# Cross-attention kernel: row statistics on ScalarE instead of VectorE, one constant row on GpSimd

## Chip, cores, metric

One core of a Trainium2 chip runs the program; the time is the device time of one execution in microseconds. Three runs of the kernel before took 2336.01, 2340.18 and 2342.96 us: median 2340.18 us. The profiled execution took 2341.09 us, of which its profile spans 2339.3 us.

## What is computed

Two layers on `x` and a context `ctx`, both 8 batches of 512 rows by 2048 channels, all float32. This study concerns the first layer and its input normalization:

```
xn = (x - mean(x)) / sqrt(var(x) + eps)          # over the 2048 channels of a row
corr = ifft(fft(xn) * conj(fft(ctx))).real       # along the 512 rows, per channel
w, idx = top_k(corr, 12);  w = softmax(w)        # per channel
out[l] = sum_i w[i] * ctx[min(idx[i] + l, 511)]  # "clamped shift" of ctx
x = x + out
```

A second layer (layer norm, 64 experts of rank 8, top 16 gate) follows on tiles of 128 rows. The change does not touch it.

## The kernel before

The transforms along the rows are written as matrix products with fixed tables. The work is cut into 32 groups: 8 batches (`B`) times 4 quarters of 512 channels (`GPB` = 4). A software pipeline runs 33 steps `i`; every engine has a hand-written order of work within `body(k, r, a, b, f, s)`, `i = 4k + 3 + r`. In step `i` the forward half handles group `i` (flag `a`) and the backward half handles group `i-1` (flag `b`). So there is no planner: what an engine does next is the next line of its own `body`, and semaphores tie the engines together.

**TensorE in a step** (from L627): the ctx transform of group `i` (`ctx_cyclic`, L533, then `ctx_negacyclic`, L557, four pairs of matmuls n = 0 to 3 into two evacuation banks), between them the x transform (`x_spectrum`, L543); the turned weights of group `i-1` (L568); the correlation of tiles 0 and 1 (L585); the weight spectrum of group `i-1` in four blocks (L601); the correlation of tiles 2 and 3; the 12 `out_row` matmuls (L623). Of these, `out_row(0, 2)` waits for `dc_put`.

**VectorE in a step** (L913 to L990): four products for the x spectrum; `evac_sin(0)` and `evac_sin(1)` (L847), which empty an evacuation bank that TensorE wants back for n = 3 and for the turned weights; the constant row ("dc", L923: row 0 of `v_cyc` gets `L * v_last`); four `w_lo`; the sums of tiles 0 and 1; the eight products of the weight spectrum; then the top-k of tiles 0 and 1, `choose` (L891) of them, the sums and top-k of tiles 2 and 3, the attention output and `choose_last`. `choose(t)` waits for the exponentials of ScalarE: `exp_done`.

**Row statistics.** A row's mean and variance must be there before its first quarter is normalized, so they are gathered two batches ahead: one quarter per step is loaded into `stat_in`, VectorE takes `bn_stats` of its four 128-row tiles (`statistics`, L736; two tiles after `evac_sin(0)`, two before the products of the weight spectrum), and in every fourth step (r = 3, that is i = 2, 6, ... 26; called a means step below) `means` (L742) aggregates them, ScalarE takes the root (`root`, L1082), VectorE inverts (`invert`, L775, after the second block's products) and GpSimd finishes `rstd` and `shift` (`normalizers`, L1316). ScalarE's `norm` (L1071) of group `i+2` waits for these in a means step. Steps from i = 27 on gather no statistics.

**ScalarE in a step** (L1153 to L1230): evacuations and negated copies, `w_hi`, the odd copies of tiles 0 and 1, `norm` of group `i+2`, then `dc_put` (L1205: the constant row into `r_f`, after GpSimd's third sum of products), then `big_exp` and `top_exp` of tiles 0 and 1 (L1144, L1148), the odd copies of tiles 2 and 3, `weigh`, and the copy of the attention output.

**GpSimd in a step** (L1358): the folds of the weights, first half of the x fold, the sums of products of the x spectrum, second half of the x fold (L1291, L1292), first op of the ctx fold (L1297), four sums of products of the weight spectrum, rest of the ctx fold.

**SyncE's queue** issues in order: x of group `i+2`, ctx of group `i+1`, its last row (`load_last`), `stat_in`, the store of the attention output.

The order on ScalarE that the change writes into:

```
                if i + 2 < GROUPS:
                    norm_inputs(k, r, 2)
                    norm(k, r, 2, range(LT))
                ...
                if b:
                    act.wait_ge(add_done, prod_w(i, 2) + 1)
                    act.wait_ge(dc_ready, i)
                    nc.scalar.activation(r_f[0:1, 0, :], ...).then_inc(dc_put, 1)
                if a:
                    for t in (0, 1):
                        big_exp(i, t)
```

Of the kernel before, what the change touches and what calls it, by code (L numbers as in the profile page):

```python
# [129 lines left out]
def build_program(nc, x, ctx, a_w, b_w, wq_w, keys, tables, out):  # L130
# [6 lines left out]
    with ExitStack() as st:  # L137
# [13 lines left out]
        def sem(name):  # L151
            return st.enter_context(nc.semaphore(name))


        ident, pace = sb("ident", [P, P]), sb("pace", [P, 32])
        bn_x, norm_x = sb("bn_x", [P, LT, GPB, 6]), [sb(f"norm_x{n}", [P, LT, 2]) for n in range(2)]
        rstd2, shift2 = sb("rstd2", [P, TT]), sb("shift2", [P, TT])
# [6 lines left out]
        xfs[1], vf = sb("xf1", [P, 4, CH]), sb("vf", [P, 4, CH])  # L164
        fwd, v_last = sb("fwd", [P, 13, P]), sb("v_last", [P, CH])
        v_cyc[0], v_neg[0] = sb("v_cyc0", [P, 6, CH]), sb("v_neg0", [P, 6, CH])
# [40 lines left out]
            sem("tables_loaded"), sem("fwd_loaded"), sem("tables_split"), sem("x0_half"))  # L207
        stat_loaded, stat_used = sem("stat_loaded"), sem("stat_used")
        norm_step, root_done, norm_ready = sem("norm_step"), sem("root_done"), sem("norm_ready")
        consts_set = sem("consts_set")  # L210
# [3 lines left out]
        evac_ready, evac_act, evac_dve, minus_done = sem("evac_ready"), sem("evac_act"), sem("evac_dve"), sem("minus_done")  # L214
        dc_ready, dc_put = sem("dc_ready"), sem("dc_put")
        w_hi_done, w_lo_done = sem("w_hi_done"), sem("w_lo_done")
# [137 lines left out]
        def _(sp):  # L354
# [28 lines left out]
            def body(k, r, a, b, f, s):  # L383
                i = 4 * k + 3 + r

                if i + 2 < GROUPS:
                    sp.wait_ge(pair_ready, pair_x(i, 1) + 1)
                    load_x(k, r, 2)
                if f:
                    sp.wait_ge(evac_ready, evac_neg(i, 3) + 1)  # L390
                    load_v(k, r, 1)
                    sp.wait_ge(dc_ready, i + 1)
                    load_last(k, r, 1)
                if is_step(i, 0):
                    sp.wait_ge(stat_used, LT * 2)
                    load_stat(k, r, stat_in[:], stat_loaded)
                if (i - 2) // GPB + 2 < B:
                    sp.wait_ge(stat_used, LT * (i + 3))
                    load_stat((i - 2) // GPB, (i - 2) % GPB, stat_in[:], stat_loaded)
                if is_step(i, GROUPS - 1):  # L400
                    last_group(i)
                if is_step(i, GROUPS):
                    last_step(i)
                if b:
                    sp.wait_ge(att_done, i)
                    sp.dma_start(at_group(att_t, k, r, -1), att_sb[:]).then_inc(stored, 16)
# [24 lines left out]
            def last_group(i):  # L431

                sp.wait_ge(stored, 16 * GPB)
                sp.wait_ge(pair_ready, pair_x(i - 1, 1) + 1)
                sp.wait_ge(stat_used, LT * (1 + GPB * (B - 1)))
                for h in range(2):
                    load_rows(0, 0, h)
                load_others(0, 0, 0)
                sp.wait_ge(v_ready, i + 1)
                for h in range(2):  # L440
                    load_rows(0, 1, h)
                sp.wait_ge(pair_ready, pair_x(i, 1) + 1)
                load_part(0)
                sp.wait_ge(evac_ready, evac_neg(i, 3) + 1)
                sp.wait_ge(dc_ready, i + 1)
                load_part(1)
                load_part(2)
                load_others(0, 0, 1)
                sp.wait_ge(prod_ready, prod_w(i, 3) + 1)
                sp.wait_ge(dc_put, i)  # L450
                load_part(3)
                load_others(0, 1, 0)
# [275 lines left out]
        def _(dve):  # L728
# [13 lines left out]
            def means(m):  # L742

                if not is_step(m, 0):
                    hold(norm_ready, NORM_OPS * m)
                for j in range(LT):
                    nc.vector.bn_aggr(norm_x[0][:, j, :], bn_x[:, j, :, :].rearrange("p g s -> p (g s)")).then_inc(norm_step, 1)

            def first_normalizers():
# [81 lines left out]
            def body(k, r, a, b, f, s):  # L831
# [75 lines left out]

                def first_statistics():
                    if not is_step(i, 0):
                        dve.wait_ge(stat_loaded, 16 * (i + 2))  # L910
                        statistics(stat_in, r, i, (0, 1))

                if a:  # L913
# [5 lines left out]
                    evac_sin(0)  # L919
                    if s:  # L920
                        first_statistics()
                    evac_sin(1)
                    nc.vector.scalar_tensor_tensor(v_cyc[cur][0:1, 0, :], v_last[0:1, :], float(L), v_cyc[cur][0:1, 0, :],  # L923
                                                   ALU.mult, ALU.add).then_inc(dc_ready, 1)
                    if is_step(i, 0):
                        dve.wait_ge(stat_loaded, 16)
                        statistics(stat_in, 0, 0)
                        dve.wait_ge(tables_split, 1)
# [10 lines left out]
                if a:  # L939
                    sums_of((0, 1))  # L940
                if s and not is_step(i, 0):
                    statistics(stat_in, r, i, (2, 3))
                    if r == 3:
                        hold(stat_used, LT * (i + 3))
                        means(k + 2)
                if last_step:
# [26 lines left out]
                if a:  # L973
# [4 lines left out]
                    topk_stages((2, 3), range(4))  # L978
                if is_step(i, 0):
                    dve.wait_ge(stat_loaded, 32)  # L980
                    statistics(stat_in, r, i)
                if is_step(i, GROUPS - 1):
# [87 lines left out]
        def _(act):  # L1070
# [6 lines left out]
            def norm_inputs(k, r, off):  # L1077
                g = 4 * k + 3 + r + off
                act.wait_ge(x_loaded[g % 2], 16 * (g // 2))
                act.wait_ge(norm_ready, NORM_OPS * (k + quarter(r, off)[1]) + NORM_OPS)  # L1080

            def root(m):  # L1082

# [37 lines left out]
            def body(k, r, a, b, f, s):  # L1121
# [49 lines left out]
                if a:  # L1171
                    evac_from(0, evac_neg(i, 0), v_neg[cur][:, 0, :])
                    minus(v_neg[cur][:, 2, :], v_neg[cur][:, 0, :], 6 * i + 5)
                    evac_from(0, evac_neg(i, 2), v_neg[cur][:, 3, :])
                    minus(v_neg[cur][:, 5, :], v_neg[cur][:, 3, :], 6 * i + 6)
# [12 lines left out]
                if i + 2 < GROUPS:  # L1188
                    norm_inputs(k, r, 2)
                    norm(k, r, 2, range(LT))  # L1190
                if is_step(i, GROUPS):
                    act.wait_ge(prod_ready, prod_w(i - 1, 3) + 1)
# [13 lines left out]
                if a:  # L1206
# [5 lines left out]
                    for t in (0, 1):  # L1212
                        weigh(i, t)
                if is_step(i, GROUPS - 1):
                    for t in (2, 3):
# [61 lines left out]
        def _(pool):  # L1277
# [80 lines left out]
            def body(k, r, a, b, f, s):  # L1358
# [11 lines left out]
                if a:  # L1370
                    if not is_step(i, 0):
                        pool.wait_ge(lag_ready, CT * i)
                    for n in range(2):
                        add_products(prod_x(i, n), n, p_f[:, 2 * n:2 * n + 2, :])
                if is_step(i, GROUPS - 1):
                    add_half(0, 0, 0, 0)
# [68 lines left out]
```

## Time and profile before

| | |
|---|---|
| median of 3 runs | 2340.18 us (2336.01 to 2342.96) |
| profiled execution | 2341.09 us, span 2339.3 us |
| busy: TensorE, VectorE, GpSimd, ScalarE | 2265.3, 1874.8, 1567.8, 1031.9 us |
| chain that ended last | TensorE 88%, VectorE 9% |
| mean granted clock | 0.991 of full speed |

The attention layer takes the first 1440 us or so, the second layer the rest. An engine's busy time alone does not say whether it sets the pace: TensorE's matmuls overlap, so its line is nearly full either way. The chain of waits says which instruction the next one waited for; the distance between the same instruction of two steps says what a step takes.

### The profile page before, as it was taken

To read this page: it belongs to the slowest core of one execution; us is meant where nothing else is said; L and a number is where in the kernel's file an instruction comes from. 1 tells how busy PE (TensorE), PEld (TensorE's weight loads), DVE (VectorE), ACT (ScalarE), POOL (GpSimd) and SP (SyncE) were. 2 spreads that over 40 slices of the span, in tenths; PEclk is the share of its full clock that TensorE was granted. 3 is DMA by queue.
4 is the path that set the end of the run, shared out by engine and by line. 5 is a ranking of instruction groups with operands and counts; after the bars stand their busy time and mean duration, and the time that the engine had idled before them with its cause. 6 is when DMAs were issued, how large, how long until landed. Compare 5 with 4: busy or idle time off the path is not lost.

```text
span 2339.3 us, 29526 instructions
## 1 busy us (share of the span) xinstructions
PE 2265.3 (97%) x9664; PEld 1549.1 (66%) x9664; DVE 1874.8 (80%) x3947; ACT 1031.9 (44%) x1872; POOL 1567.8 (67%) x997
## 2 busy tenths in 40 slices
PE   4999999999999999999999998799999999999999
PEld 2566566566556656656656655577778777887787
DVE  6999999999999999999998998765656566666652
ACT  3453453453454454454454444444444443444441
POOL 4998998998998898898998986523343333333330
PEclk9999999999999999999999998899999999999999
DMA  6232232232233233233222125534444444444431
GB/s 227 95 117 95 93 119 95 84 125 98 77 113 117 77 113 117 77 113 114 80 87 89 59 80 201 197 126 163 159 160 166 161 152 161 170 155 152 160 126 54
DMA packets 110413, 288.04 MB, mean 123 GB/s; under 512 B 7136, under 2 KB 7264, under 8 KB 109152
## 3 DMA queue, kind: packets, MB, share of 16 engines
q1 hardware_dynamic: 110304, 286.72, 35.7%
q8 instruction: 53, 0.87, 0.1%
q14 instruction: 56, 0.46, 0.1%
HBM read 219.58 MB, written 67.11 MB: 123 GB/s over the span
## 4 chain that ended last, share of the span: by engine, by line
PE 88%; DVE 9%; DMA 1%; issue 1%; ACT 1%; POOL 1%; SPq 0%; DVEq 0%; ACTq 0%
PE pair L625 14%; PE lag L597 7%; PE out L499 6%; PE out L501 5%; PE out L500 5%; PE evac L541 5%; PE z L499 5%; PE z L501 5%; PE evac L566 5%; PE pair L554 5%; PE evac L565 5%; PE z L500 5%; PE pair L499 4%; PE pair L500 4%; PE pair L501 4%; PE tp L511 2%
## 5 line engine op out<-in xcount | busy, mean ns | idle before, releaser
L1307 POOL TENSOR_TENSOR r_f<-prod 128x1024 f32<-128x1024 f32 x128 | 303.8, 2384 | 120.6 <-DVE prod L845 77.7
L1341 POOL TENSOR_TENSOR rows<-rows,cin 128x1024 f32<-128x1024 f32 x48 | 115.7, 2411 | 363.9 <-DMA rows<-out_dram 294.3
L625 PE MATMUL pair<-r_f,back 128*128 128x512 f32 x768 | 335.4, 592 | 0.0
L625 PEld LDWEIGHTS pair<-r_f,back 128*128 128x128 f32 x768 | 145.7, 190 | 169.4 <-issue 167.8
L597 PE MATMUL lag<-lags,p_f 128*128 128x256 f32 x1024 | 233.1, 381 | 3.4 <-DVE e L866 2.6
L499 PE MATMUL pair<-w_hi,wts_hi 128*128 128x512 f32 x512 | 210.0, 410 | 9.8 <-DVE prod L845 7.2
L597 PEld LDWEIGHTS lag<-lags,p_f 128*128 128x128 f32 x1024 | 192.8, 191 | 30.6 <-issue 4.6
L499 PE MATMUL out<-b_hi,zt_hi 128*128 128x512 f32 x512 | 209.6, 409 | 1.6 <-ACT zt_hi L1250 1.5
L499 PE MATMUL z<-a_hi,xt 128*128 128x512 f32 x512 | 206.5, 403 | 0.4 <-DVE a_lo L795 0.4
L500 PE MATMUL pair<-w_lo,wts_hi 128*128 128x512 f32 x512 | 200.9, 392 | 0.0
L501 PE MATMUL out<-b_hi,zt_lo 128*128 128x512 f32 x512 | 200.8, 392 | 0.0
L500 PE MATMUL out<-b_lo,zt_hi 128*128 128x512 f32 x512 | 200.7, 392 | 0.0
L501 PE MATMUL pair<-w_hi,wts_lo 128*128 128x512 f32 x512 | 200.5, 392 | 0.0
L501 PE MATMUL z<-a_hi,xt 128*128 128x512 f32 x512 | 200.4, 391 | 0.0
L500 PE MATMUL z<-a_lo,xt 128*128 128x512 f32 x512 | 199.6, 390 | 0.0
L802 DVE TENSOR_TENSOR xt<-tp,xt 128x512 fp32r<-128x512 f32 x128 | 88.4, 691 | 128.5 <-ACT xt L1102 128.5
L1100 ACT ACTIVATE xt_full<-tp 128x512 f32<-128x512 f32 x128 | 75.9, 593 | 246.4 <-PE score_sums L524 132.7
L1344 POOL TENSOR_TENSOR rows<-xin,rows 128x1024 f32<-128x1024 f32 x64 | 159.9, 2498 | 12.1 <-DMA xin<-in_x_dram 2.6
L541 PE MATMUL evac<-vf,fwd 128*128 128x512 f32 x256 | 125.0, 626 | 33.3 <-POOL vf L1354 26.5
L845 DVE TENSOR_TENSOR prod<-pair,v_cyc 128x1024 f32<-128x1024 f32 x128 | 155.4, 1214 | 0.0
L1307 POOL TENSOR_TENSOR p_f<-prod 128x1024 f32<-128x1024 f32 x64 | 149.8, 2364 | 0.0
L1039 DVE SCALAR_TENSOR_TENSOR rows<-out,rows 128x512 f32<-128x512 f32 x128 | 87.8, 686 | 60.3 <-PE out L501 58.9
(157 smaller groups left out, 5422.9 us busy)
## 6 DMA issues: line engine op xcount, KB each, us to landing
vf<-in_ctx_dram SPq DMA_DIRECT2D x32, 1024.0 KB, 5.1
out_dram<-att_sb SPq DMA_DIRECT2D x32, 1024.0 KB, 4.2
rows<-out_dram SPq DMA_DIRECT2D x64, 512.0 KB, 3.6
cin<-out_dram SPq DMA_DIRECT2D x64, 512.0 KB, 4.1
xin<-in_x_dram SPq DMA_DIRECT2D x64, 512.0 KB, 3.9
out_dram<-rows SPq DMA_DIRECT2D x64, 512.0 KB, 2.6
xf<-in_x_dram SPq DMA_DIRECT2D x30, 1024.0 KB, 5.1
stat_in<-in_x_dram SPq DMA_DIRECT2D x28, 1024.0 KB, 5.1
```

Of the source, the lines that this page charges most:

```text
L499: nc.tensor.matmul(out, lhs_hi, rhs_hi, start=start, stop=False)
L500: nc.tensor.matmul(out, lhs_hi, rhs_lo, start=False, stop=False)
L501: return nc.tensor.matmul(out, lhs_lo, rhs_hi, start=False, stop=stop)
L541: nc.tensor.matmul(evac_ps[n % 2][:], fwd[:, n, :], vf[:, fold, :], start=True, stop=True).then_inc(evac_ready, 1)
L554: last = nc.tensor.matmul(pair_ps[:, 2 * n + part, :], fwd[:, t, :], xfs[i % 2][:, fold, :], start=True, stop=True)
L565: nc.tensor.matmul(evac_ps[n % 2][:], fwd[:, t, :], vf[:, first, :], start=True, stop=False)
L566: nc.tensor.matmul(evac_ps[n % 2][:], fwd[:, t + 1, :], vf[:, second, :], start=False, stop=True).then_inc(evac_ready, 1)
L597: last = nc.tensor.matmul(lag_ps[t % 2][:, cols], p_f[:, 2 * par + part, ch], lags[:, par, cols], start=par == 0, stop=par == 1)
L625: return nc.tensor.matmul(pair_ps[:, bank, :], back[:, 3 * bank + n, :], r_f[:, row, :], start=n == 0, stop=n == 2)
L845: nc.vector.tensor_tensor(slot[:, 2:4, :], s_ps, vs[:, 1:3, :], ALU.mult).then_inc(prod_ready, 1)
L1307: nc.gpsimd.tensor_tensor(dst, prod[:, slot, 0:2, :], prod[:, slot, 2:4, :], ALU.add).then_inc(add_done, 1)
L1344: nc.gpsimd.tensor_tensor(half, xin[:], half, ALU.add).then_inc(x2_added, 1)
```

## The change

The diff moves the row statistics from VectorE to ScalarE. For each tile of a loaded quarter ScalarE makes a `Copy` with an accumulated sum and a `Square` about an approximate mean (that of the batch's first quarter) with an accumulated sum, both in place: eight ACTIVATEs per group (`row_sums`, `row_squares`), placed behind `norm` and ahead of `dc_put` and the exponentials. A quarter is taken one step later in the pipeline's numbering of groups (group `i+2` in step i, counted from 0 for batch 1's first quarter), its load is issued in the step before, and steps 0 and 1 take two quarters each. In the means step six small VectorE instructions replace the four `bn_aggr`. The constant row becomes a scaled copy of the last row on ScalarE (`dc_last`) and an addition of one row on GpSimd, behind the sums of products of the x spectrum.

```
@@ SyncE
-                    sp.wait_ge(dc_ready, i + 1)
+                    sp.wait_ge(dc_scaled, i + 1)
+                    sp.wait_ge(evac_dve, 2 * i + 2)
                     load_last(k, r, 1)
-                if is_step(i, 0):
-                    sp.wait_ge(stat_used, LT * 2)
-                    load_stat(k, r, stat_in[:], stat_loaded)
-                if (i - 2) // GPB + 2 < B:
-                    sp.wait_ge(stat_used, LT * (i + 3))
-                    load_stat((i - 2) // GPB, (i - 2) % GPB, stat_in[:], stat_loaded)
+                for g in (1, 2) if is_step(i, 0) else (3, 4) if is_step(i, 1) else (i + 3,):
+                    if g < GPB * (B - 1):
+                        sp.wait_ge(stat_used, LT * (g + 1))
+                        load_stat(g // GPB - 1, g % GPB, stat_in[:], stat_loaded)
@@ VectorE
+            def later_means(m):
+                mean, var = norm_x[0][:, :, 0], norm_x[0][:, :, 1]
+                sums, squares, off, off_square = (total_x[:, n, :] for n in range(4))
+                done = 4 * (m - 1)
+                dve.wait_ge(stat_used, LT * (GPB * m + 1))
+                nc.vector.tensor_reduce(sums, sum_x[:], mybir.AxisListType.X, ALU.add).then_inc(mean_step, 1)
+                nc.vector.tensor_reduce(squares, square_x[:], mybir.AxisListType.X, ALU.add).then_inc(mean_step, 1)
+                dve.wait_ge(mean_step, done + 2)
+                nc.vector.scalar_tensor_tensor(off, sums, 1.0 / D, near_mean[:], ALU.mult, ALU.add).then_inc(mean_step, 1)
+                dve.wait_ge(norm_ready, NORM_OPS * m)
+                nc.vector.tensor_scalar(mean, sums, 1.0 / D, None, ALU.mult).then_inc(norm_step, 1)
+                dve.wait_ge(mean_step, done + 3)
+                nc.vector.tensor_tensor(off_square, off, off, ALU.mult).then_inc(mean_step, 1)
+                dve.wait_ge(mean_step, done + 4)
+                nc.vector.scalar_tensor_tensor(var, squares, 1.0 / D, off_square, ALU.mult, ALU.subtract).then_inc(norm_step, LT - 1)
...
                     evac_sin(0)
-                    if s:
-                        first_statistics()
                     evac_sin(1)
-                    nc.vector.scalar_tensor_tensor(v_cyc[cur][0:1, 0, :], v_last[0:1, :], float(L), v_cyc[cur][0:1, 0, :],
-                                                   ALU.mult, ALU.add).then_inc(dc_ready, 1)
                     if is_step(i, 0):
-                        dve.wait_ge(stat_loaded, 16)
-                        statistics(stat_in, 0, 0)
...
                     sums_of((0, 1))
-                if s and not is_step(i, 0):
-                    statistics(stat_in, r, i, (2, 3))
-                    if r == 3:
-                        hold(stat_used, LT * (i + 3))
-                        means(k + 2)
+                if s and r == 3:
+                    later_means(k + 2)
...
-                if is_step(i, 0):
-                    dve.wait_ge(stat_loaded, 32)
-                    statistics(stat_in, r, i)
@@ ScalarE
+            def row_sums(g):
+                act.wait_ge(stat_loaded, 16 * (g + 1))
+                if g % GPB == 0 and g > 0:
+                    act.wait_ge(norm_step, NORM_STEPS * (g // GPB) + LT)
+                for j in range(LT):
+                    nc.scalar.activation(stat_in[:, j, :], stat_in[:, j, :], ACT.Copy,
+                                         accum_out=sum_x[:, j, g % GPB:g % GPB + 1]).then_inc(stat_summed, 1)
+                if g % GPB == 0:
+                    act.wait_ge(stat_summed, LT * (g + 1))
+                    nc.scalar.activation(near_mean[:], sum_x[:, :, 0], ACT.Copy, scale=-1.0 / CH).then_inc(near_done, 1)
+            def row_squares(g):
+                act.wait_ge(stat_summed, LT * (g + 1))
+                act.wait_ge(near_done, g // GPB + 1)
+                for j in range(LT):
+                    nc.scalar.activation(stat_in[:, j, :], stat_in[:, j, :], ACT.Square, bias=near_mean[:, j:j + 1],
+                                         accum_out=square_x[:, j, g % GPB:g % GPB + 1]).then_inc(stat_used, 1)
...
                     evac_from(0, evac_neg(i, 0), v_neg[cur][:, 0, :])
+                    act.wait_ge(last_loaded, 16 * (i + 1))
+                    if not is_step(i, 0):
+                        act.wait_ge(dc_ready, i)
+                    nc.scalar.activation(dc_last[:], v_last[0:1, :], ACT.Copy, scale=float(L)).then_inc(dc_scaled, 1)
                     minus(v_neg[cur][:, 2, :], v_neg[cur][:, 0, :], 6 * i + 5)
...
                     norm(k, r, 2, range(LT))
+                if is_step(i, 0):
+                    row_sums(0)
+                    row_squares(0)
+                elif is_step(i, 1):
+                    row_sums(2)
+                    row_squares(2)
+                if i > 0 and i + 2 < GPB * (B - 1):
+                    row_sums(i + 2)
+                    row_squares(i + 2)
...
                     for t in (0, 1):
                         weigh(i, t)
+                if is_step(i, 0):
+                    row_sums(1)
+                    row_squares(1)
@@ GpSimd
                         add_products(prod_x(i, n), n, p_f[:, 2 * n:2 * n + 2, :])
+                    pool.wait_ge(dc_scaled, i + 1)
+                    dc = v_cyc[(r + 1) % 2][0:1, 0, :]
+                    nc.gpsimd.tensor_tensor(dc, dc, dc_last[:], ALU.add).then_inc(dc_ready, 1)
```

Two small tiles and the semaphores that go with this are added as well; the loads of the second layer's first weights wait for `evac_dve` in place of `evac_ready` (same point of the step).

## Rows read from the trace of the kernel before

**Rows 1.** The page, busy times (share of the span), and its chain by engine.
```profile
PE 2265.3 (97%) x9664; PEld 1549.1 (66%) x9664; DVE 1874.8 (80%) x3947; ACT 1031.9 (44%) x1872; POOL 1567.8 (67%) x997
PE 88%; DVE 9%; DMA 1%; issue 1%; ACT 1%; POOL 1%; SPq 0%; DVEq 0%; ACTq 0%
```
**Rows 2.** Windows of one step each: window, us, busy by engine, clock, DMA share, GB/s.
```profile
98.48:143.23 44.75, 44.09 (x153) 27.24 (x153) 41.87 (x93) 21.40 (x44) 40.02 (x32) 1.00 0.31 101
143.23:187.30 44.07, 44.06 (x153) 27.25 (x153) 41.28 (x86) 21.52 (x42) 39.49 (x27) 1.00 0.30 102
541.32:587.72 46.40, 44.31 (x154) 27.16 (x153) 43.55 (x86) 19.96 (x40) 39.07 (x27) 1.00 0.28 97
1251.36:1295.14 43.78, 43.78 (x153) 27.20 (x153) 39.01 (x82) 19.96 (x40) 39.35 (x27) 1.00 0.23 78
```
**Rows 3.** Chain of waits, in order of time: start us, us, what.
```profile
98.48 10.30 PE pair L625 x24
...
566.30 5.01 DVE v_cyc L923
...
1207.57 10.30 PE pair L625 x24
```
**Rows 4.** Instructions of a line: min/median/max ns, first and last start us.
```profile
L923 DVE SCALAR_TENSOR_TENSOR v_cyc<-v_last,v_cyc x32: 673/2782/5091, 47.4 to 1407.6; 1x512 f32<-1x512 f32 x32
L826 DVE SCALAR_TENSOR_TENSOR rstd<-norm_x x32: 158/2218/2343, 1456.7 to 2274.2; 128x1 f32 x24, 128x1 f32<-128x1 f32 x8
```
**Rows 5.** Groups of instructions on ScalarE and GpSimd: busy us, mean ns.
```profile
L1132 ACT ACTIVATE v_cyc<-v_cyc 128x512 f32<-128x512 f32 x64 | 36.5, 622 | 0.0
L1146 ACT ACTIVATE e<-e,neg_max 128x512 f32<-128x512 f32 x128 | 86.3, 716 | 44.6 <-DVE pick L877 44.5
L1150 ACT ACTIVATION_READ_ACCUMULATOR exp_top<-top,neg_max 128x1 f32 x128 | 23.9, 187 | 0.0
L1313 POOL TENSOR_TENSOR pick<-e 128x255 f32<-128x255 f32 x128 | 93.3, 729 | 0.0
```
**Rows 6.** Timeline of ScalarE, parts of a normal step, then of the means step i = 14.
```profile
603.02 1.14 ACT L1132 ACTIVATE v_cyc<-v_cyc 128x512 f32<-128x512 f32 x2
630.50 0.63 ACT L1205 ACTIVATE r_f<-v_cyc 1x512 f32<-1x512 f32 x1 [10.15 <-POOL r_f L1307]
632.86 1.38 ACT L1146 ACTIVATE e<-e,neg_max 128x512 f32<-128x512 f32 x2 [1.72 <-DVE pick L877]
...
673.54 2.93 ACT L1075 ACTIVATE xf<-xf,shift,rstd 128x512 f32<-128x512 f32 x4 [6.54 <-POOL shift L1330]
...
677.00 1.28 ACT L1146 ACT_TABLE_LOAD   x1
678.30 1.34 ACT L1146 ACTIVATE e<-e,neg_max 128x512 f32<-128x512 f32 x2
679.54 0.29 ACT L1150 ACTIVATE exp_top<-top,neg_max 128x12 f32<-128x12 f32 x1
```
**Rows 7.** Timelines of GpSimd, VectorE and TensorE, same means step and the next.
```profile
661.84 2.40 POOL L1297 TENSOR_TENSOR half_fold<-vf 128x1024 f32<-128x1024 f32 x1
664.97 1.16 DVE L844 TENSOR_TENSOR prod<-pair,v_neg 128x1024 f32<-128x1024 f32 x1
680.96 0.15 DVE L893 RECIPROCAL inv_sum<-exp_sum 128x1 f32<-128x1 f32 x1
697.34 0.75 DVE L854 SCALAR_TENSOR_TENSOR v_neg<-v_last,ones,evac 128x512 f32<-128x512 f32 x1
698.85 1.02 PE L565 MATMUL evac<-vf,fwd 128*128 128x512 f32 x2
```
**Rows 8.** ScalarE in steps 0 and 1, and the page's row of a load: us to landing.
```profile
54.38 1.28 ACT L1146 ACT_TABLE_LOAD   x1
64.53 0.60 ACT L1128 ACTIVATE v_cyc<-evac 128x512 f32<-128x512 f32 x1 [2.92 <-PE evac L541]
stat_in<-in_x_dram SPq DMA_DIRECT2D x28, 1024.0 KB, 5.1
```

More of the change, by code:

```diff
@@ L155, in build_program @@
         ident, pace = sb("ident", [P, P]), sb("pace", [P, 32])
+        sum_x, square_x = sb("sum_x", [P, LT, GPB]), sb("square_x", [P, LT, GPB])
+        total_x, near_mean = sb("total_x", [P, 4, LT]), sb("near_mean", [P, LT])
         bn_x, norm_x = sb("bn_x", [P, LT, GPB, 6]), [sb(f"norm_x{n}", [P, LT, 2]) for n in range(2)]
@@ L164, in build_program @@
         xfs[1], vf = sb("xf1", [P, 4, CH]), sb("vf", [P, 4, CH])
-        fwd, v_last = sb("fwd", [P, 13, P]), sb("v_last", [P, CH])
+        fwd, v_last, dc_last = sb("fwd", [P, 13, P]), sb("v_last", [P, CH]), sb("dc_last", [1, CH])
         v_cyc[0], v_neg[0] = sb("v_cyc0", [P, 6, CH]), sb("v_neg0", [P, 6, CH])
@@ L208, in build_program @@
         stat_loaded, stat_used = sem("stat_loaded"), sem("stat_used")
+        stat_summed, near_done, mean_step = sem("stat_summed"), sem("near_done"), sem("mean_step")
         norm_step, root_done, norm_ready = sem("norm_step"), sem("root_done"), sem("norm_ready")
@@ L214, in build_program @@
         evac_ready, evac_act, evac_dve, minus_done = sem("evac_ready"), sem("evac_act"), sem("evac_dve"), sem("minus_done")
-        dc_ready, dc_put = sem("dc_ready"), sem("dc_put")
+        dc_scaled, dc_ready, dc_put = sem("dc_scaled"), sem("dc_ready"), sem("dc_put")
         w_hi_done, w_lo_done = sem("w_hi_done"), sem("w_lo_done")
@@ L443, in last_group @@
                 load_part(0)
-                sp.wait_ge(evac_ready, evac_neg(i, 3) + 1)
+                sp.wait_ge(evac_dve, 2 * i + 2)
                 sp.wait_ge(dc_ready, i + 1)
@@ L742, in means @@
             def means(m):
-                if not is_step(m, 0):
-                    hold(norm_ready, NORM_OPS * m)
                 for j in range(LT):
                     nc.vector.bn_aggr(norm_x[0][:, j, :], bn_x[:, j, :, :].rearrange("p g s -> p (g s)")).then_inc(norm_step, 1)
+            def later_means(m):
[13 more added lines that the diff above has]
+                nc.vector.scalar_tensor_tensor(var, squares, 1.0 / D, off_square, ALU.mult, ALU.subtract).then_inc(norm_step, LT - 1)
             def first_normalizers():
@@ L906, in choose_last @@
                         choose(t)
[L908 to L911, printed above, removed]
                 if a:
```

## The prediction

> **What bounds the kernel now.** I began with the page. TensorE is busy 97% of the span, VectorE 80%, GpSimd 67%, ScalarE 44%, and 88% of the chain that ended last is TensorE [rows 1]. That makes ScalarE look like the place with room, but a busy line does not say what a step waits for, so I went on to the length of the steps. The same matmul group starts each step's end at 98.48 and, 25 steps later, at 1207.57 us [rows 3]: 1109.1 us, or 44.4 us a step. Four windows show what differs between steps [rows 2]. One without statistics takes 43.78 us with TensorE busy for all 43.78. One with `bn_stats` takes 44.07, a means step 44.75, and one single step 46.40, in which the constant row held VectorE for 5.01 us [rows 3]. So 43.79 us is TensorE's own work, the floor. Everything that VectorE costs in these 25 steps is 1109.1 - 25 x 43.79 = 14.3 us: 18 steps with 0.3, 7 means steps with about 0.95, 2.4 for the long one. **No relief of VectorE can give back more than about 14 us here**, plus little in step 0.
>
> VectorE is tight for another reason: its order. In the means step i = 14 it starts `choose(0)` at 680.96, and `evac_sin(0)` of the next step at 697.34 ends at 698.09; between the two it had no idle time of note. TensorE wants that bank at 698.85 [rows 7]. So from `choose(0)` on the slack is 0.76 us. `choose(0)` itself waits for ScalarE's small exponential, which ends at 679.9 (679.54, plus its accumulator read) [rows 6]: slack 1.04 us. Together 1.80 us. What ScalarE is late in a means step beyond 1.8 us, TensorE pays in the next step.
>
> **The change, part by part.**
>
> *VectorE loses* four `bn_stats` and the constant row in each step that has them. The constant row is dear, 673 to 5091 ns with a median of 2782 [rows 4], for one partition of 512 elements. Its price is mostly waiting for a GpSimd instruction. All of it is worth the 14.3 us above and no more, as TensorE's floor stands next.
>
> *ScalarE gains* eight ACTIVATEs a group. Two negated copies, SBUF to SBUF, took 1.14 us [rows 6] at 622 ns each [rows 5], so they follow each other after 0.51. Squares have a bias from a tile, as the big exponentials, 716 ns each [rows 5] and two in 1.34 [rows 6], so after 0.64. The accumulator read lasts 187 ns [rows 5]; two pairs with it in the trace overlap it by half, so I add 0.09 each. 4 x 0.60 + 4 x 0.73 is 5.3, with 0.2 for the drain between sums and squares 5.5, and with the approximate mean (every fourth group, the means steps) 5.8 us. The lower bound is eight copies at 0.51, 4.1 us; the upper is eight of 716 + 187 ns and the mean, 7.5 us. I take 5.5 and 5.8, nearest to the same shapes.
>
> *In a normal step* this lies in 10.15 us in which ScalarE waits for GpSimd before `dc_put` [rows 6]. It costs nothing; if the block were over 10 us it would delay `dc_put` and the exponentials.
>
> *In a means step* that cover is gone. `norm` itself waits 6.54 us for GpSimd's `shift`, starts at 673.54 and ends at 676.4; the table load for Exp comes at 677.00 and the exponentials at 678.30 [rows 6]. ScalarE is back to back here. The block stands between `norm` and these, and moves them by 5.8 us. `dc_put` still just makes it: it ends near 41.7 us into the step, and TensorE asks for it at 40.4 (counted from the step's first matmul: 43.79 less the last third of the 10.30 us of L625 [rows 3]) plus that step's own stall. The exponentials do not: 5.8 - 1.8 = 4.0 us of TensorE stall in the following step, shared out between the bank of the attention output, the evacuations of ctx and `evac_sin(0)`. This happens in the steps i = 2, 6, ... 22, six times (i = 26 gathers nothing more): **24.0 us**. By the bounds of the block 2.3 to 5.7 us each.
>
> The Trainium skill speaks of a dearer switch here. The table load in the trace lasts 1.28 us and the exponential starts 0.02 after it [rows 6]. "ScalarE: Activation LUTs", What ACT_TABLE_LOAD costs, puts a switch at about 2.66 us, load and drain. If `Square` needed a table of its own, that figure would add some 2.7 us to each block, an estimate by the page; by the row it would add 1.3. I take none, as the kernel's copies run between exponentials without a load.
>
> *The means on VectorE.* Before, products of the weight spectrum began at 664.97 in the means step [rows 7], 0.95 late for the floor. Now six small instructions stand there, three of which read two SBUF operands. Such an instruction on a 128x1 tile took 158 ns at best and 2218 in the median [rows 4] while GpSimd was at work. They come about 20.7 us into the step, when GpSimd is in L1297, 2.40 us long, from 661.84 [rows 7]. The new one-row addition on GpSimd shifts that by 0.8: its price is between 729 ns (255 elements [rows 5]) and twice that; by elements 1.24, less the 0.45 for which GpSimd waited for VectorE's constant row. So the first of the small ones gets through at 665.0, the three behind it need 0.65, and the products begin 0.8 later than before. Lower bound: no collision, 0.2 late for the floor; upper: 2.4 late. I take 1.7, by the row of L1297: 7 x 1.7 = **11.9 us**.
>
> The Trainium skill bears on the six: "SBUF — State Buffer", Who interferes with whom, lets a VectorE instruction with two SBUF inputs contend with GpSimd reads, and never a `tensor_reduce`. By that rule only the later ones can be caught, which agrees with L826; if nothing could be caught, this term would be near 1.4 us.
>
> *GpSimd's* addition (1.24 us a step) falls ahead of the 2 to 3 us that it waits for products; nothing follows. Uncovered it would be 32 x 0.8. *SyncE's queue:* the `stat_in` load waits for ScalarE's squares, in a means step till about 41 us into it; behind it is only the store of the output, due later, and the x load of the next step. The 1 MB load lands in 5.1 us [rows 8], a step ahead of need: nothing. *ScalarE's one-row copy*, 0.63 us, lies in an idle gap of some 2 us before the next evacuation: nothing.
>
> *Start.* In step 0 the table load came at 54.38, right behind `norm` [rows 8]; now a block of 5.8 comes between, then exponentials, then the block of group 1, then step 1's first evacuation. That stood at 64.53 [rows 8]. I get: block to 60.2, load 61.5, exponentials and odd copies to 63.9, `weigh` behind `choose` to 65.1, `stat_in` landed at 65.3, block to 70.7: TensorE's third ctx matmul is **6.0 us** late net. In step 1 two blocks and a landing between them take 5.5 + 5.2 + 5.5 = 16.2 where a normal step has 12.5 (10.15 + 0.63 + 1.72 [rows 6]) before the exponentials; with `dc_put` they are 4.3 late. Slack in a normal step is 0.7 greater (678.30 - 632.86 against the means step's length), 2.5: **1.8 us**. Bounds of the two together: 3 to 14.
>
> **Sum.** The floor plus 24.0 + 11.9 + 6.0 + 1.8 = 43.7 against the floor plus 14.3 before: +29.4 us. The profiled execution took 2341.09, 0.9 above the median of the three runs; 2341.1 + 29.4 = 2370.5, or 2369.6 by the median. I predict **2370 us**. A measurement of this kernel can tell about 0.3%, 7 us, from no change.
>
> **Rivals.**
> 1. *Faster: VectorE's relief decides.* The mechanism is the constant row leaving VectorE. Place: before `w_lo`. It decides if the exponentials of the means step are not held up, that is if ScalarE's block there costs under 1.8 us, or `norm` is released some 4 us earlier. Then all 14.3 goes and 0 to 2 us of step 0 with it: 2326 to 2329. For it: VectorE is 94% busy in the attention and the 5.01 us collision ends. Against: [rows 6], back to back ACTIVATEs; and the price of eight of them has no row near 1.8.
> 2. *No measurable change.* The relief comes, but the start (+7.8) and the small instructions (7 x 1.0) eat it, while VectorE makes up part of the late exponentials, having shed the constant row's 2.78 us and four `bn_stats` a step. 2341 - 14.3 + 7.8 + 7 = 2341.5. Against: the shed work lies after `evac_sin(0)`, so behind the place at which TensorE waits.
> 3. *Much slower.* Blocks at their upper bound, small instructions caught twice, and TensorE's granted clock, 1.00 in all windows of rows 2, falling after the stalls: 2385 to 2395.
> 4. *The change does not do what it says*: VectorE's busy share falls, but TensorE sets the pace anyway. That is contained in the 14.3.
>
> **How the numbers follow.** Slower as worked out, with rival 3: 0.70. Faster, rival 1: 0.16, as the slack of 1.8 us is read off one step. No change: 0.14. Lower ends of all terms give 2344 and upper ends 2392; with most of rival 2 the range is 2336 to 2392, the slower case's own 2346 to 2392.
>
> **What would show it.** Right: means steps at about 45.5 us, the step after them at about 47.8, all others at 43.8; in a means step the exponentials at some 42.9 us behind its first matmul, VectorE idle before L893's reciprocal for 4 to 5 us "by ScalarE"; VectorE's busy time down by the 89 us of constant rows (32 x 2.78) and its `bn_stats`, ScalarE's up by some 28 x 5.5 = 150; first evacuation of step 1 near 70.7. Wrong: means cycles of 4 x 43.8 us, or exponentials that follow `norm` at once; blocks under 3 us; or losses in normal steps, which would point to GpSimd or the load queue.

## The result, and the profile after

The changed kernel takes **2371.49 us** (median of 4 runs, 2370.97 to 2372.34) against 2340.81 us of the kernel before (2336.01 to 2342.96): ratio 1.0134, 95% interval 1.0117 to 1.0152. The forecast was 2370 us, slower. Its profiled execution took 2370.97 us, span 2369.2, 29.9 more than before.

The changed kernel's page, busy times and the chain by engine:

```profile
PE 2264.3 (96%) x9664; PEld 1545.3 (65%) x9664; DVE 1737.4 (73%) x3803; ACT 1196.8 (51%) x2359; POOL 1595.2 (67%) x1029
PE 81%; DVE 8%; ACT 5%; issue 3%; POOL 2%; DMA 1%; DVEq 0%; SPq 0%; ACTq 0%; POOLq 0%
```

Against [rows 1], VectorE sheds 137 us of work and ScalarE gains 165; TensorE works as much as before. By busy times alone this reads as a good trade. The chain says otherwise: ScalarE had 1% of it and now has 5%.

Windows of the changed kernel, each from the start of a step's out_row matmuls to that of a later step (window, us, busy by engine, granted clock, DMA share, GB/s): a normal step, two steps that hold a means step (i = 6) and the one behind it, and the last means step (i = 26), which gathers no statistics on ScalarE:

```profile
244.60:288.41 43.81, 43.81 (x153) 27.21 (x153) 36.49 (x81) 25.75 (x57) 40.15 (x28) 1.00 0.30 102
288.41:381.64 93.23, 88.52 (x305) 54.24 (x305) 75.79 (x168) 54.81 (x120) 81.17 (x60) 1.00 0.28 96
1192.67:1238.15 45.48, 44.06 (x154) 27.25 (x153) 39.24 (x88) 21.77 (x45) 40.76 (x33) 1.00 0.22 76
```

A normal step is at TensorE's floor, 43.79 us, the time of its own matmuls ([rows 2] had 44.07). The pair takes 93.23 - 2 x 43.79 = 5.65 us more than two floors; 1.7 and 4.0, together 5.7, were forecast for it. The last means step is 1.69 above the floor, forecast 1.7. The granted clock is 1.00 in all three, so none of this is clock.

Where the 4.0 us arise shows on the timelines of the means step i = 6. ScalarE, start us, us, engine, line and operation, and in brackets its idle time before and who ended it (some lines left out):

```profile
330.92 2.93 ACT L1075 ACTIVATE xf<-xf,shift,rstd 128x512 f32<-128x512 f32 x4 [6.82 <-POOL shift L1366]
333.75 0.62 ACT L1088 ACTIVATE stat_in<-stat_in 128x512 f32<-128x512 f32 x1
...
336.33 0.21 ACT L1092 ACTIVATE near_mean<-sum_x 128x4 f32<-128x4 f32 x1
336.63 0.72 ACT L1099 ACTIVATE stat_in<-stat_in,near_mean 128x512 f32<-128x512 f32 x1
...
339.46 0.61 ACT L1238 ACTIVATE r_f<-v_cyc 1x512 f32<-1x512 f32 x1
340.09 1.28 ACT L1166 ACT_TABLE_LOAD   x1
341.39 1.33 ACT L1166 ACTIVATE e<-e,neg_max 128x512 f32<-128x512 f32 x2
```

and VectorE, same step, the small instructions and the reciprocal of `choose(0)`:

```profile
319.25 0.16 DVE L755 TENSOR_REDUCE total_x<-sum_x 128x4 f32<-128x16 f32 x1
319.33 0.16 DVE L756 TENSOR_REDUCE total_x<-square_x 128x4 f32<-128x16 f32 x1
319.52 2.15 DVE L758 SCALAR_TENSOR_TENSOR total_x<-total_x,near_mean 128x4 f32<-128x4 f32 x1
...
322.29 1.23 DVE L861 TENSOR_TENSOR prod<-pair,v_neg 128x1024 f32<-128x1024 f32 x1
...
343.04 0.16 DVE L910 RECIPROCAL inv_sum<-exp_sum 128x1 f32<-128x1 f32 x1 [4.65 <-ACT exp_top L1170]
```

In [rows 6] the table load came 3.46 us behind the start of `norm`, with `dc_put` (0.61 us) between. Now 5.71 us of statistics lie between as well (333.75 to 339.46), and VectorE stands idle for 4.65 us before a reciprocal for which it did not wait at all in [rows 7]. Above it, an instruction on 4 elements a partition takes 2.15 us (319.52).

### The profile page after: what moved, and what is told of

It is laid out like the page before. It is cut to its first block, busy times and chain, and to the rows that moved or that the text cites. A ratio compares the mean times of both kernels' runs of the same rounds, so it can differ in the third digit from the quotient of the medians.

```text
span 2369.2 us, 30004 instructions
## 1 busy us (share of the span) xinstructions
PE 2264.3 (96%) x9664; PEld 1545.3 (65%) x9664; DVE 1737.4 (73%) x3803; ACT 1196.8 (51%) x2359; POOL 1595.2 (67%) x1029
## 4 chain that ended last, share of the span: by engine, by line
PE 81%; DVE 8%; ACT 5%; issue 3%; POOL 2%; DMA 1%; DVEq 0%; SPq 0%; ACTq 0%; POOLq 0%
PE pair L627 10%; PE lag L599 8%; PE out L501 6%; PE out L503 5%; PE out L502 5%; PE z L501 5%; PE z L503 5%; PE z L502 5%; PE evac L567 4%; PE evac L568 4%; PE pair L501 4%; PE pair L503 4%; PE pair L502 4%; PE evac L543 4%; PE pair L556 4%
## 5 line engine op out<-in xcount | busy, mean ns | idle before, releaser
L1348 POOL TENSOR_TENSOR pick<-e 128x255 f32<-128x255 f32 x128 | 93.2, 728 | 73.1 <-ACT e L1157 73.1
```

## The experiments

All of them are compared with the kernel before on their own chip. Medians of that kernel differ between chips (2341.1 us beside runs 1 to 4, 2347.8 beside 5 to 7, 2344.3 beside 8 and 9, 2355.0 beside 10 and 11); the two versions that ran on two chips moved by 1 and 2 us, so the absolute times are compared with the forecasts and the ratios with 1.

**1. The block ahead of norm in the means steps.** ScalarE waits there anyway.

```
                 if s and r == 3:
                     root(k + 2)
+                    if i + 2 < GPB * (B - 1):
+                        row_sums(i + 2)
+                        row_squares(i + 2)
...
-                if i > 0 and i + 2 < GPB * (B - 1):
+                if i > 0 and r != 3 and i + 2 < GPB * (B - 1):
```

> The changed kernel, but in the means steps ScalarE's eight statistics ACTIVATEs stand right behind the root, ahead of norm, where it waits 6.82 us for GpSimd's shift. Theory (late exponentials, 4.0 us of TensorE stall in each of six cycles): the block of 5.8 us fits in the wait, the exponentials follow norm again, 24 us come back: 2347 us, and the pair of steps that took 93.23 us takes about 89.3. Rival A (the small VectorE instructions behind GpSimd's lock are the loss): 2371, nothing changes. Rival B (ScalarE's added load as such slows the step, wherever it stands): 2365 to 2371.

Measured: **2347.21 us**, ratio 1.0025 (1.0015 to 1.0035). ScalarE's timeline of a means step of this version:

```profile
496.35 0.21 ACT L1109 ACTIVATE norm_x<-norm_x 128x4 f32<-128x4 f32 x1
496.46 0.61 ACT L1088 ACTIVATE stat_in<-stat_in 128x512 f32<-128x512 f32 x1
...
503.39 2.93 ACT L1075 ACTIVATE xf<-xf,shift,rstd 128x512 f32<-128x512 f32 x4 [1.11 <-POOL shift L1369]
506.22 0.61 ACT L1241 ACTIVATE r_f<-v_cyc 1x512 f32<-1x512 f32 x1
506.85 1.28 ACT L1166 ACT_TABLE_LOAD   x1
```

The block fits with 1.11 us to spare. The same windows as above:

```profile
460.90:506.34 45.44, 44.05 (x154) 27.24 (x153) 39.21 (x88) 27.34 (x62) 40.72 (x33) 1.00 0.28 96
506.34:550.15 43.81, 43.81 (x154) 27.20 (x153) 36.59 (x81) 27.36 (x59) 40.37 (x28) 1.00 0.31 106
```

The step behind the means step is at the floor, the means step itself still 1.65 above it. The same work on the same engine, in another place, takes 24.3 us less; both rivals fall.

**2. The constant row alone.** The kernel before, with that row on ScalarE and GpSimd and its `bn_stats` untouched:

```
-                    nc.vector.scalar_tensor_tensor(v_cyc[cur][0:1, 0, :], v_last[0:1, :], float(L), ...)
+                    nc.scalar.activation(dc_last[:], v_last[0:1, :], ACT.Copy, scale=float(L)).then_inc(dc_scaled, 1)
...
+                    nc.gpsimd.tensor_tensor(dc, dc, dc_last[:], ALU.add).then_inc(dc_ready, 1)
...
```

> The kernel before, with only the constant row moved (scaled copy on ScalarE, addition on GpSimd); statistics stay on VectorE. Theory: VectorE's products of the weight spectrum come 2.7 us earlier, so that a step with bn_stats is within 0.05 us of TensorE's floor of 43.79 and a means step within 0.7; the 46.40 us step goes: of the 14.3 us that VectorE cost before, 8.5 come back: 2332 us. Rival (GpSimd's extra 1.27 us a step costs what it brings, as GpSimd is 89% busy here): 2341, or slower by some us.

Measured: **2329.98 us**, ratio 0.9948 (0.9930 to 0.9966). Windows of a means step and a step with `bn_stats`:

```profile
99.03:143.28 44.25, 44.05 (x153) 27.24 (x153) 39.44 (x92) 21.77 (x45) 40.71 (x33) 1.00 0.30 102
143.28:187.08 43.80, 43.80 (x154) 27.19 (x153) 38.92 (x85) 21.95 (x43) 40.33 (x28) 1.00 0.30 103
```

So with four `bn_stats` on VectorE a step is already at the floor. The constant row was what pushed VectorE over; there was nothing left for the moved statistics to give but 0.46 us in a means step. My 0.7 for that step was a little high, which is the 2 us between 2332 and 2330.

**3. The statistics alone.** The changed kernel, with the constant row back on VectorE behind `evac_sin(1)`:

```
                     evac_sin(1)
+                    nc.vector.scalar_tensor_tensor(v_cyc[cur][0:1, 0, :], v_last[0:1, :], float(L), ...).then_inc(dc_ready, 1)
...
-                    nc.scalar.activation(dc_last[:], v_last[0:1, :], ACT.Copy, scale=float(L)).then_inc(dc_scaled, 1)
...
-                    nc.gpsimd.tensor_tensor(dc, dc, dc_last[:], ALU.add).then_inc(dc_ready, 1)
```

> The changed kernel, but the constant row is back on VectorE. Theory: the 4.0 us stalls stay (6 x 4.0), the means steps are 0.94 late and not 1.7 (GpSimd's fold comes 0.8 earlier), now and then a constant row waits 5 us: 2366 to 2368. Rival (the loss comes from GpSimd's added row): about 2340 or less.

Measured: **2366.99 us** (2365.38 to 2369.41), ratio 1.0104 (1.0085 to 1.0122). A usual pair, one with a long constant row, and the last means step:

```profile
286.89:379.37 92.48, 88.54 (x305) 54.19 (x305) 79.46 (x170) 54.02 (x118) 79.65 (x58) 1.00 0.29 97
827.33:922.95 95.62, 90.31 (x306) 55.17 (x305) 81.13 (x170) 54.01 (x118) 79.41 (x58) 0.98 0.28 94
1190.98:1235.65 44.67, 44.06 (x153) 27.24 (x153) 40.40 (x89) 21.06 (x43) 39.70 (x32) 1.00 0.23 77
```

The means step is 0.88 above the floor (0.94 expected), a pair 4.9; the pair with the long row (5.11 us, at 852.23) takes 3.1 more. So the 4.0 us stalls come from the statistics, as the step behind the means step still takes 47.8. GpSimd's added row has a small part in the other term: without it a means step is 0.81 us shorter (0.88 in place of 1.69).

**4. Shorter blocks in the means steps.**

```
+                c = slice(0, P if g % GPB == 0 and g > 0 else CH)
                 for j in range(LT):
-                    nc.scalar.activation(stat_in[:, j, :], stat_in[:, j, :], ACT.Copy,
+                    nc.scalar.activation(stat_in[:, j, c], stat_in[:, j, c], ACT.Copy,
```

and the same in `row_squares`.

> The changed kernel, but in the six means steps ScalarE's eight ACTIVATEs cover 128 of a tile's 512 columns (so the sums of that quarter leave out three quarters of the channels). Block 3.2 us in place of 5.8. Theory, with a slack of 1.8 us ahead of which nothing is lost: 1.4 of stall in place of 4.0, six times: 2371.5 - 15.3 = 2356. If the slack were zero, the same 15.3 less but a stall of 3.2 left in the trace; if the loss does not hang on the block's length: 2371.

Measured: **2356.70 us**, ratio 1.0063 (1.0044 to 1.0081).

```profile
285.33:375.98 90.65, 88.41 (x306) 54.27 (x305) 75.75 (x168) 52.20 (x120) 81.15 (x60) 1.00 0.30 99
```

The pair is 2.58 us shorter than 93.23, and the block is 3.15 us long in this trace (330.68 to 333.83) where it was 5.71: one for one. Of the pair's 3.07 us above two floors 1.7 are the means step's, so 1.4 of stall stay for a block of 3.2 us. The slack is 1.8 us, the value that the prediction had read from one step.

**5. The small VectorE instructions between the evacuations.** VectorE waits 2.69 us there.

```
                     evac_sin(0)
+                    if s and r == 3:
+                        later_means(k + 2)
                     evac_sin(1)
...
-                if s and r == 3:
-                    later_means(k + 2)
```

> The changed kernel, but the six small VectorE instructions of a means step stand between the two evacuations (evac_sin), where VectorE waits 2.7 us for TensorE, in place of right ahead of the products. Theory (they make the means steps 1.7 us late, by one wait for a GpSimd fold and their own length, seven times): 11.9 less, 2360; means steps fall from 45.5 to about 43.9 us while the 4.0 us of the step behind stay. Rival (the 1.7 us come from ScalarE's late root or block, not from these): 2371, means steps still 45.5.

Measured: **2420.61 us**, ratio 1.0307 (1.0289 to 1.0325): 49 us slower where 12 faster was expected. Timelines of a means step on VectorE, GpSimd and TensorE:

```profile
317.07 0.77 DVE L758 SCALAR_TENSOR_TENSOR total_x<-total_x,near_mean 128x4 f32<-128x4 f32 x1
317.77 2.40 DVE L760 TENSOR_SCALAR norm_x<-total_x 128x4 f32<-128x4 f32 x1
320.07 0.15 DVE L762 TENSOR_TENSOR total_x<-total_x 128x4 f32<-128x4 f32 x1
320.33 5.65 DVE L764 SCALAR_TENSOR_TENSOR norm_x<-total_x 128x4 f32<-128x4 f32 x1
```
```profile
315.46 4.68 POOL L1343 TENSOR_TENSOR p_f<-prod 128x1024 f32<-128x1024 f32 x2
320.09 1.27 POOL L1413 TENSOR_TENSOR v_cyc<-v_cyc,dc_last 1x512 f32<-1x512 f32 x1
321.33 2.33 POOL L1327 TENSOR_TENSOR xf<-half_fold 128x1024 f32<-128x1024 f32 x1
323.62 2.33 POOL L1328 TENSOR_TENSOR xf<-half_fold 128x1024 f32<-128x1024 f32 x1
326.10 2.35 POOL L1333 TENSOR_TENSOR half_fold<-vf 128x1024 f32<-128x1024 f32 x1
```
```profile
326.69 1.12 PE L584 MATMUL evac<-ident,pick 128*128 128x128 f32 x4 [5.85 <-DVE v_neg L871]
327.60 5.74 PE L599 MATMUL lag<-lags,p_f 128*128 128x256 f32 x16
```

I had counted one wait. There are two long ones: 2.40 us, to the end of the GpSimd instruction that ran, and 5.65 us. The last of the small instructions began at 320.33 and ended at 325.98, over three GpSimd instructions that follow each other without a pause; the third ended at 325.95 and the next began at 326.10. TensorE was 5.85 us idle, and its granted clock then fell to the slower level: windows of this stretch show 0.50 from 325 to 331 us (1.2 GHz). The correlation takes 5.4 us (327.60 to 332.99) where it takes 3.5 in a normal step.

```profile
319.00:325.00 6.00, 1.84 (x14) 1.32 (x12) 5.90 (x3) 1.69 (x4) 6.00 (x4) 1.00 0.52 175
325.00:331.00 6.00, 4.31 (x12) 3.61 (x13) 4.12 (x6) 0.60 (x1) 3.30 (x2) 0.50 0.19 44
```

Neither theory nor rival had this. The move trades one wait for two and a stretch at the low clock, in all seven means steps.

**6. The first batch's statistics on VectorE.** Groups 0 to 3 go through `bn_stats` as before (steps 0 to 2), ScalarE starts with group 4:

```
+                    if i in (1, 2):
+                        dve.wait_ge(stat_loaded, 16 * (i + 2))
+                        statistics(stat_in, r, i, (0, 1))
...
-                if is_step(i, 0):
-                    row_sums(0)
-                    row_squares(0)
-                elif is_step(i, 1):
-                    row_sums(2)
-                    row_squares(2)
```

and the matching lines of steps 0 to 2.

> The changed kernel, but the statistics of batch 1 (groups 0 to 3, steps 0 to 2) stay on VectorE as before; ScalarE takes them from batch 2 on. Theory: the start gives back its 6.0 + 1.8 us, and the means step i = 2 one more (bn_aggr in place of the small instructions): 2363; the first out_row group of step 1 comes near 98 us as before. Rival (the start costs nothing, the loss is all in the later cycles): 2370 to 2371.

Measured: **2363.46 us**, ratio 1.0062 (1.0045 to 1.0080), 8.0 us less than the changed kernel. Step 1's `out_row` matmuls start at 99.07 us (98.48 in the kernel before).

**7. The edits of runs 1, 5 and 6 together.** This forecast was made before the result of the fifth run.

> All three edits on the changed kernel: block ahead of norm in the means steps, small VectorE instructions between the evacuations, batch 1 on VectorE. Theory: the losses are additive terms of 24.0, 11.2 and 7.8 us, all steps from 3 on at TensorE's floor of 43.8: 2328 us, faster than the kernel before by some 12 us and at least level with the constant row alone (2330). Rival (a next wait takes their place, for instance the root that now has to wait for GpSimd's lock, or the block that fits its gap by under 1 us): 2335 to 2345.

Measured: **2380.04 us**, ratio 1.0131 (1.0113 to 1.0149). That is 52 us off the forecast, for the same reason as run 5: a means step takes 52.03 us, 8.2 above the floor, at a clock of 0.93, and the step behind it 43.81.

```profile
275.50:327.53 52.03, 46.18 (x154) 28.82 (x153) 45.55 (x88) 27.12 (x61) 40.44 (x33) 0.93 0.27 87
327.53:371.34 43.81, 43.81 (x153) 27.19 (x153) 36.58 (x81) 27.66 (x60) 40.66 (x28) 1.00 0.31 102
```

**8. The edits of runs 1 and 6**, the small instructions back in their place.

> Two of the three edits: block ahead of norm in the means steps and batch 1 on VectorE; the six small instructions are back where the changed kernel has them. Theory (terms add; in the run with all three the small instructions alone were to blame, being caught by several GpSimd instructions in a row): the 2347.2 of the first edit less 7.8 of the start and 1.0 of step 2: 2338.5, level with the kernel before. Rival (the two edits get in each other's way in step 2, or the start is worth less once the cycles are mended): 2342 to 2347.

Measured: **2338.14 us**, ratio 0.9968 (0.9953 to 0.9983). The terms add up. Against the seventh run, the place of six small instructions in six steps makes 41.9 us.

**9. The small arithmetic on GpSimd.** As run 8; VectorE keeps the two `tensor_reduce`:

```
+                    if s and r == 3 and i > 2:
+                        pool_means(k + 2)
...
-                nc.vector.scalar_tensor_tensor(off, sums, 1.0 / D, near_mean[:], ALU.mult, ALU.add)
+                nc.gpsimd.tensor_scalar(mean, sums, 1.0 / D, None, ALU.mult).then_inc(norm_step, 1)
+                nc.gpsimd.tensor_scalar(squares, squares, 1.0 / D, None, ALU.mult).then_inc(mean_step, 1)
...
+                nc.gpsimd.tensor_tensor(off, mean, near_mean[:], ALU.add).then_inc(mean_step, 1)
...
```

> As the run before it, and the small arithmetic of the means steps moves from VectorE to GpSimd (five instructions of some 0.28 us behind its first op of the ctx fold, where it waits for products); VectorE keeps the two tensor_reduce. Theory: no VectorE instruction with two SBUF operands is left in these steps, the 1.7 us of six means steps go, 10.2 less: 2328, all steps near 43.8; the first tensor_reduces are not held up by GpSimd. Rival (the root, now behind GpSimd's fold, pushes ScalarE's block past the gap ahead of norm, and the exponentials are late by over 1.8 us again): 2333 to 2345, with means steps mended and the step behind them long.

Measured: **2327.98 us** (2326.96 to 2329.16), ratio 0.9919 (0.9900 to 0.9938). The first instruction of this arithmetic took 2150 ns on VectorE, waiting for GpSimd's fold (L1332 here, L1333 in the changed kernel). Its counterpart on GpSimd stands behind the same fold and takes about 0.2 us:

```profile
304.55 2.40 POOL L1332 TENSOR_TENSOR half_fold<-vf 128x1024 f32<-128x1024 f32 x1
306.90 0.24 POOL L1374 TENSOR_SCALAR norm_x<-total_x 128x4 f32<-128x4 f32 x1
```

The rival's delay is there, but small: `shift` is ready at 314.72, ScalarE's block ends after it, and `norm` starts at 315.69. That is 1.0 us late, inside the slack of 1.8.

**10 and 11. The two fastest beside each other**: the kernels of run 2 and run 9 again, on one chip.

> The kernel with only the constant row moved, again, on one chip with the run that moved the small arithmetic to GpSimd as well. By their steps it has 24 to 25 us over 25 floors less: seven means steps at 44.25 in place of 43.79, all other steps at the floor: 3.2 us over it. Expected 2330, ratio to the kernel before 0.995.

> The kernel with block ahead of norm, batch 1 on VectorE and the small arithmetic on GpSimd, again, beside the one with the constant row alone. If all of its steps but the first means step are at the floor, it is some 3 us ahead of it, 2327 to 2328. If moving the statistics brings nothing beyond the constant row, the two are level within 1 us.

Measured: 2331.82 us (2330.16 to 2333.05), ratio 0.9909 (0.9878 to 0.9940), and 2328.89 us (2327.63 to 2330.21), ratio 0.9895 (0.9865 to 0.9926). The kernel before took 2355.02 on this chip, so its ratios are not those of the earlier calls. The version of run 9 is 2.9 us ahead of the constant row alone, by medians whose ranges just touch; in run 2 and run 9, on two chips, it was 2.0. That is the whole worth of moving the statistics, once nothing is lost by it: six means steps at the floor that had been 0.46 above it, 2.8 us.

## Why the prediction was right, point by point

- **The floor and the 14.3 us.** Normal steps came at 43.81 us, and no step with both halves was shorter than 43.7 in any version. The gain was bounded as forecast: the 25 steps between the two groups of [rows 3] took 14.3 us above their floors before, and take 1.0 in run 9.
- **The block.** Forecast 5.8 us, measured 5.71 (333.75 to 339.46). With its accumulator read a `Copy` follows the one before after 0.61 us (0.60 forecast) and a `Square` after 0.71 (0.73). No table load for `Square`: the table loads in the trace are those of before, so the Trainium skill's dearer switch ("ScalarE: Activation LUTs", What ACT_TABLE_LOAD costs) had no part here; the load that there is again lasts 1.28 us and its exponential starts 0.02 later. That switch takes 1.30 us here (340.09 to 341.39), not the 2.66 that the Trainium skill gives.
- **Its place.** 4.0 us for each of six cycles: 24.0 forecast, 24.3 by run 1, and run 4 gives the slack of 1.8 us. VectorE's wait for the exponential, 4 to 5 us forecast, is 4.65; the exponentials start 42.8 us behind the step's first matmul (298.55 to 341.39), forecast 42.9.
- **The small instructions.** 1.7 us a means step forecast, 1.69 measured. The mechanism held in the place where they stand: the first that reads two SBUF operands is caught once, by L1333. That it "gets through" when the running instruction ends was in part luck of the place, as run 5 shows. GpSimd pauses for 3.13 us behind L1333. Where its next instruction follows at once, the wait can go on, and my upper bound of 2.4 us for such a group was too low as a general price.
- **The one-row addition on GpSimd.** Forecast 1.24 us, measured 1.27. It is hidden in normal steps, and its 0.8 in a means step is part of the 1.7: run 3, without it, has 0.81 less.
- **The start.** First evacuation of step 1 forecast at 70.7, measured at 70.44; step 1's `out_row` at 105.47 against 98.31 before (timelines of TensorE), so 7.2 us where I had 6.0. TensorE ran the ctx and x transforms of step 1 at a lower clock than before (0.82 granted from 71 to 86 us, against 0.94 from 65 to 80), which I had left out. Whether that is the whole difference one execution cannot tell: the same kernel had this group at 97.93 in run 9 and at 100.16 in run 11. Step 2's share was 1.9 (1.8 forecast). Run 6 gives 8.0 for both with step 2's microsecond (8.8 forecast).
- **Sum.** +29.4 forecast, +29.9 by the spans. Terms measured one by one come to 24.0 + 11.8 + 7.2 + 1.9 - 14.3 = 30.6. The steps show where the rest is: the last interval between two `out_row` groups took 1.27 us less than before and the work behind it 0.52 more. That interval varies without any change, 38.30 in run 2 and 36.80 in run 10 with one and the same kernel, so no effect of this change can be read from it.
- **Busy times.** VectorE's fell by 137 us. ScalarE's rose by 165 where 150 stood in the forecast; that counted the statistics alone, and the 32 one-row copies are 19.6 us more.
- **The rival "faster"** failed on its condition: the block costs 5.7 us and not under 1.8. Once it was moved to where ScalarE waits, and the rest mended, the gain of that rival (2326 to 2329) is what came out: 2328. Nearly all of that comes from the constant row, as run 2 shows, and about 2 to 3 us from the statistics.

## What to carry to other kernels

Relieving an engine gives back at most what the steps take above the floor of the engine that bounds them, and that can be read from steps that lack the work in question. Work that moves onto an engine with much idle time has to land in the idle time: the same eight instructions cost 0 us in a normal step, 4 us in a step where that engine's wait comes earlier in its order, and 0 again in that step when they stand ahead of `norm`, inside the wait. Before moving several things at once, time each alone; here one one-row instruction held 11 of the 14 us.

## What the runs showed that I had not expected

A VectorE instruction that meets a busy GpSimd is mostly served when the running GpSimd instruction ends, but not always, if the next one follows at once. The constant row before shows both. 30 times it met L1291 with L1292 right behind. In 29 of these it got in between the two, after 2.65 to 2.79 us, and L1292 became longer; once it had to wait for L1292 as well, and took 5.09 us:

```profile
566.09 2.37 POOL L1291 TENSOR_TENSOR xf<-half_fold 128x1024 f32<-128x1024 f32 x1
568.42 2.35 POOL L1292 TENSOR_TENSOR xf<-half_fold 128x1024 f32<-128x1024 f32 x1
...
612.49 2.36 POOL L1291 TENSOR_TENSOR xf<-half_fold 128x1024 f32<-128x1024 f32 x1
614.82 2.81 POOL L1292 TENSOR_TENSOR xf<-half_fold 128x1024 f32<-128x1024 f32 x1
```
```profile
566.22 5.09 DVE L923 SCALAR_TENSOR_TENSOR v_cyc<-v_last,v_cyc 1x512 f32<-1x512 f32 x1
...
612.62 2.78 DVE L923 SCALAR_TENSOR_TENSOR v_cyc<-v_last,v_cyc 1x512 f32<-1x512 f32 x1
```

In run 5 the last small instruction waited over three in a row, 5.65 us for 4 elements a partition, seven times out of seven (5641 to 5651 ns), while the first of the same group got in between two back-to-back GpSimd instructions after 0.77 us. What decides between being served and waiting on stays open. The Trainium skill ("SBUF — State Buffer", Who interferes with whom) says that whoever issues first gets the shared pair for the whole instruction and the other blocks; the trace agrees, and adds that the waiting side can lose several times over. A `TENSOR_SCALAR` with one SBUF operand took 2.40 us in run 5, to the end of the GpSimd instruction that ran, while the `TENSOR_REDUCE`s took 0.16 us in both places with GpSimd at work. The kernel before also varies more from run to run and chip to chip than the versions without the constant row on VectorE. A long row costs its step 2.3 us (46.40 against 44.1), so these waits may be the reason, but that was not tried by itself.
